# Routed-row scatters held behind TensorE signals, in a decoder layer with mixture-of-experts routing on one Trainium2 core

## What is computed

```
x = x + linear_attention_block(layernorm(x))        # incl. its own FFN with gelu
x = x + cross_attention(layernorm(x), ctx)          # 16 heads of 8, 77 keys a batch, softmax
x = x + moe(layernorm(x))
# moe: logits = xf @ gate_w.T; probs = softmax; top_p, top_i = top_k(probs, 2)
#      w = top_p / sum(top_p); rank = running count of tokens per (expert, choice)
#      keep = rank < capacity (1280); for each of 8 experts:
#      out += comb[:, e] * (silu(xf @ gate_e.T) * (xf @ up_e.T)) @ down_e.T
```

## Time and profile before

| | us |
|---|---|
| median of 3 runs (lowest, highest) | 974.47 (972.26, 980.99) |
| the profiled execution's own time | 977.34 |
| its span, first to last instruction | 975.5 |
| mean granted TensorE clock, share of full speed | 0.943 |
| TensorE matmul busy | 844.6 (87%) |
| VectorE busy | 641.7 (66%) |
| GpSimd busy | 539.9 (55%) |
| ScalarE busy | 453.3 (46%) |
| the 128 scatters of L852, busy on GpSimd | 129.6 |

### The profile page before, as it was taken

One profiled execution on the slowest core, in us unless ns is written; L12 is line 12 of the kernel. 1 busy time (PEld: TensorE's weight loads), 2 busy tenths in 40 slices (PEclk: granted clock), 3 DMA queues, 4 the chain that ended last, 5 costly groups with the idle time before them and its releaser, 6 DMA issues.

```text
span 975.5 us, 25508 instructions
## 1 busy us (share of the span) xinstructions
PE 844.6 (87%) x9107; PEld 625.8 (64%) x9107; DVE 641.7 (66%) x2064; ACT 453.3 (46%) x708; POOL 539.9 (55%) x747
## 2 busy tenths in 40 slices
PE   4799999999999999999999999862789889979883
PEld 3577787787667776666766667741456656656661
DVE  5888988988567877777777776734244544434443
ACT  1466766766367666666666655521222222222220
POOL 3465665665532366666655655565356656565565
PEclk8899999999999999999999998955799999989997
DMA  6369930000000011110000000100433344546440
GB/s 234 98 238 390 388 123 0 0 1 1 1 2 14 25 58 57 57 41 31 28 28 30 28 30 26 55 29 32 156 106 131 115 134 108 157 126 198 135 154 3
DMA packets 50336, 87.01 MB, mean 89 GB/s; under 512 B 12809, under 2 KB 28105, under 8 KB 50232
## 3 DMA queue, kind: packets, MB, share of 16 engines
q1 hardware_dynamic: 37872, 72.18, 22.0%
q0 software_dynamic: 11264, 12.70, 4.0%
q10 hardware_dynamic: 1096, 0.73, 0.2%
HBM read 42.08 MB, written 58.41 MB: 103 GB/s over the span
## 4 chain that ended last, share of the span: by engine, by line
PE 48%; DVE 8%; another core or an unknown queue 8%; issue 7%; ACT 3%; POOL 2%; DMA 1%; DVEq 0%; SPq 0%; POOLq 0%; ACTq 0%
PE psum L1398 6%; PE psum L1418 6%; PE psum L1880 6%; PE psum L1383 5%; PE psum L1892 5%; PE psum L1388 3%; PE psum L1429 2%; PE psum L1401 2%; DVE h L1832 2%; PE psum L1365 2%; DVE yo L1817 2%; PE psum L1369 1%; ACT num L1269 1%; PE psum L626 1%
## 5 line engine op out<-in xcount | busy, mean ns | idle before, releaser
L1779 POOL DMA_INDIRECT out<-yo,token x160 | 158.7, 992 | 123.3 <-issue 108.4
L852 POOL DMA_INDIRECT dispatched<-z,idx x128 | 129.6, 1013 | 72.7 <-issue 47.0
L1261 ACT ACTIVATE PT<-psum,key_bias 77x2048 f32<-77x2048 f32 x64 | 125.5, 1961 | 74.9 <-PE psum L1401 74.9
L1861 ACT ACTIVATE act_g<-psum 128x512 f32<-128x512 f32 x80 | 46.1, 596 | 191.2 <-DVE h L1832 95.3
L1398 PE MATMUL psum<-qT,Kb 32*77 32x128 f32 x2048 | 126.8, 282 | 0.8 <-issue 0.8
L951 DVE TENSOR_REDUCE top_score<-psum 128x8 f32<-128x616 f32 x128 | 101.6, 794 | 29.7 <-PE psum L1383 27.2
L1817 DVE SCALAR_TENSOR_TENSOR yo<-psum,xin,base 128x128 f32<-128x128 f32 x156 | 44.0, 343 | 111.6 <-remote 65.6
L1892 PE MATMUL psum<-down,h 128*128 128x128 f32 x640 | 85.5, 290 | 28.9 <-DVE h L1832 24.8
L1383 PE MATMUL psum<-Kb,qT 32*128 32x308 f32 x512 | 101.5, 471 | 0.8 <-ACT z3T L1252 0.4
L1892 PEld LDWEIGHTS psum<-down,h 128*128 128x128 f32 x640 | 80.0, 203 | 33.9 <-DVE h L1832 29.3
L1401 PE MATMUL psum<-MT,minus_sel 32*77 32x128 bf16 x1024 | 97.3, 217 | 2.3 <-issue 2.3
(11 more groups left out here) (177 smaller groups left out, 1743.5 us busy)
## 6 DMA issues: line engine op xcount, KB each, us to landing
dispatched<-zeros SPq DMA_DIRECT2D x40, 522.0 KB, 7.3
xin<-dispatched SPq DMA_DIRECT2D x40, 522.0 KB
out<-zeros SPq DMA_DIRECT2D x20, 256.0 KB, 3.1
first<-out SPq DMA_DIRECT2D x20, 256.0 KB
X<-in_x SPq DMA_DIRECT2D x16, 256.0 KB, 2.6
out<-X SPq DMA_DIRECT2D x16, 256.0 KB
out<-yo,token POOLq DMA_INDIRECT x160
ctx<-in_ctxT SPq DMA_DIRECT2D x4, 616.0 KB, 6.3
```

The costliest lines, as they stand in the source:

```text
L852: pool.indirect_dma_start(xg[k], bass.IndirectOffsetOnAxis(ap=idx[n % Z4][:, t, k:k + 1], axis=0), z4[n % Z4][:, t, :], None, bounds_check ...
L1261: nc.scalar.activation(PT[j % 2][:], T.rearrange("p a c -> p (a c)"), ACT.Exp, bias=key_bias[:, bass.ds(b, 1)]).then_inc(s["PT_ready"], 1)
L1779: pool.indirect_dma_start(rows_out if slot else out, bass.IndirectOffsetOnAxis(ap=token[i][:, t:t + 1], axis=0), yo[i][:, t, :], None, bou ...
```

## The change

In the loop, the first choice's scatter now also waits for the batch's complete shifted scores (`T_ps` = 4b + 4), and the second choice's waits for the turned numerators (`OT_ps` = b) where it waited for `MT_ps` = b + 2. `add_out_bias` moves from j = 2 to j = 3. After the loop, the scatters of groups 13 and 14 each stand behind one of several TensorE signals; those of group 15 and the place of `ln_scale` of group 15 stay.

```diff
                     if group(n):
                         if j == 0:
                             scatter_ready(n)
+                        pool.wait_ge(s["T_ps"], 4 * b + 4)
                         scatter_rows(n, j, 0)
 ...
-                    if j == 2:
+                    if j == 3:
                         add_out_bias(g)
                     if group(n):
-                        if batch(b + 1):
-                            pool.wait_ge(s["MT_ps"], b + 2)
+                        pool.wait_ge(s["OT_ps"], b)
                         scatter_rows(n, j, 1)
 ...
             def last():
                 scatter_ready(NG - 3)
-                for u in range(G4):
-                    for k in range(K2):
-                        scatter_rows(NG - 3, u, k)
+                pool.wait_ge(s["T_ps"], 4 * NB)
+                scatter_rows(NG - 3, 0, 0)
+                pool.wait_ge(s["z4T_ps"], NG - 1)
+                scatter_rows(NG - 3, 0, 1)
+                pool.wait_ge(s["pv_ps"], 8 * (NB - 1))
+                scatter_rows(NG - 3, 1, 0)
+                pool.wait_ge(s["gate_ps"], NG - 1)
+                scatter_rows(NG - 3, 1, 1)
+                pool.wait_ge(s["OT_ps"], NB - 1)
+                scatter_rows(NG - 3, 2, 0)
+                pool.wait_ge(s["pv_ps"], 8 * NB)
+                scatter_rows(NG - 3, 2, 1)
+                pool.wait_ge(s["OT_ps"], NB)
+                scatter_rows(NG - 3, 3, 0)
+                pool.wait_ge(s["oT_ps"], NG)
+                scatter_rows(NG - 3, 3, 1)
                 ln_scale(NG - 1, 4, mom4, var4, rs4, shift4)
-                for n in (NG - 2, NG - 1):
-                    scatter_ready(n)
-                    for k in range(K2):
-                        for u in range(G4):
-                            scatter_rows(n, u, k)
+                scatter_ready(NG - 2)
+                scatter_rows(NG - 2, 0, 0)
+                scatter_rows(NG - 2, 1, 0)
+                pool.wait_ge(s["z4T_ps"], NG)
+                scatter_rows(NG - 2, 2, 0)
+                scatter_rows(NG - 2, 3, 0)
+                pool.wait_ge(s["gate_ps"], NG)
+                scatter_rows(NG - 2, 0, 1)
+                scatter_rows(NG - 2, 1, 1)
+                pool.wait_ge(s["rank_ps"], NG)
+                scatter_rows(NG - 2, 2, 1)
+                scatter_rows(NG - 2, 3, 1)
+                scatter_ready(NG - 1)
+                for k in range(K2):
+                    for u in range(G4):
+                        scatter_rows(NG - 1, u, k)
```

## The result

The changed kernel takes 1001.94 us (median of 4 runs, 999.04 to 1003.63) where the kernel before takes 973.59 beside it: a ratio of 1.0295, 95% interval 1.025 to 1.034. The forecast was 966.0 with a range up to 982, so the sign is wrong and the time lies far outside the range. The profiled execution took 1003.63 with a span of 1001.8, 26.3 us more than before.

What follows compares the result with a forecast made beforehand. TensorE held 48% of the chain, with scatters thought to delay its signals, 2.9 us a group. Loop -6, tail -3 and +0.5 gave -8.5 us: 977.3 to 968.8 profiled, median 966.0, range 953 to 982.

Steps and rivals of the forecast that it cites:

- Costs nothing itself: In the loop, moving add_out_bias out of j = 2 is free, since add_out needs its result only three steps later.
- V and j = 0: ScalarE's V idles well under 1 us, not 1.62; j = 0's exponential comes less than 6.5 us behind the one before.
- The exponentials of j = 1 and j = 3: Sign of being right: they come about 0.5 us later after their shifted scores began, with periods unchanged.
- signs that I had named for being right: V's short idle, j = 0's earlier exponential, later exponentials at j = 1 and 3, num's last tail wait under 5 us.
- the idle time before `num` covers the late exponentials: On ScalarE, idle of 0.59 us (j = 3) and 1.37 (j = 1) before num absorbs exponentials 0.5 us late, costing 0.
- the loop's -6 us: Over 12 loop groups, V starting sooner at j = 0 saves 0.5 us each; bounds 0 and 19 us.
- My own bound of 0.5 us for this place: Upper bound per moved second choice amid the shifted scores, where the exponentials come late; the estimate was 0.
- Rival 3: In the loop, three second choices amid the shifted scores each cost 0.5 us, 19 us in all: 987 us; chance 0.15.
- The tail: After the loop, spread scatters bring the moments 3 us sooner; group 14's scatters then come 0.5 us later.
- Rival 4: A scatter's place does nothing to TensorE; the waits only add GpSimd's lag: 975 us; chance 0.05.

Runs made afterwards that it cites:

- the residual behind: Changed kernel with add_out_bias at j = 3 moved behind the second choice's scatter, against the kernel before: 988.21 us, 1.0115 (975 kind); 906.17 us, 1.0035 (902 kind).

## Why the prediction was wrong

1. *"Costs nothing itself"*, of `add_out_bias` out of j = 2: **this is the step that failed.** I asked who needs its result, and not what runs on VectorE while it runs. I had worked out its new place, 1.0 us behind the start of the first choice of j = 3 (measured 1.16), nose to tail behind a scatter, and that place is where VectorE does the ranks of the routing. The trace of before even shows the price once, at the end of the loop, where the residual of the last group (637.75 to 639.01) and the ranks meet: the view of `taken` there has 1234 ns as its longest beside a median of 158. The runs give the meeting its price: 1.27 us a group and 12.4 us in all on the 902 kind, 17.6 us on the 975 kind, and with the residual back at j = 2 a ratio of 0.9971 instead of 1.03 on the 975 kind. On the 975 kind it takes both moves: the wait on `OT_ps` shifts it by the 1.0 us that I had worked out, and that is more than `o` has to spare once it is held.

2. *The half clock.* None of my terms had it. Before, TensorE idles 1.92 us in a group in pieces; now 1.12 us of idle time in one piece precede most falls. A full-clock group takes 25.4 us, one with 6.8 us at the lower level 27.0, so the clock is 1.6 us of the 3.1 us by which the loop's period grew. That the collision brings most of them is what the counts say: 11 and 9 stretches in the loop in the two profiles of the changed kernel on the 975 kind, six with the residual behind, none and one with it at j = 2 (the second with the old tail), and one, two and four where the loop is that of the kernel before. That the idle piece is the cause is my reading, and not a rule: on the 902 kind pieces of 0.83 us (in the group of 425.76) went by without a fall in one run, and two stretches came in another of the same kernel.

3. *V and j = 0.* Right in kind: V idles 0.29 us, and the first choice of j = 3 moved by 0.9 us in its step (3.9 to 4.8), where I had 1.0. The exponentials of j = 1 and j = 3 come about 0.5 us later after their shifted scores began (2.53 and 2.56 us, where they had 2.00 and 2.10), as forecast. So most signs that I had named for being right came, in a kernel that got slower: none of them looked at VectorE. The step table, from the first matmul of the shifted scores to the next batch's, groups at full clock:

| step | before (batches 28 to 31) | changed (20 to 23) | residual back at j = 2 (28 to 31) |
|---|---|---|---|
| j = 0 | 6.61 | 7.34 | 5.91 |
| j = 1 | 6.14 | 5.88 | 6.15 |
| j = 2 | 5.78 | 6.23 | 5.92 |
| j = 3 | 5.49 | 5.98 | 5.99 |
| sum | 24.02 | 25.43 | 23.97 |

Without the collision, j = 0 gains 0.7 us. But j = 3 loses 0.5: that the idle time before `num` covers the late exponentials was wrong as well, and so the loop's -6 us came to nothing (286.7 us from batch 12 to 60 with the residual at j = 2, 287.2 before). The exponentials were not the only thing held. With the wait alone, TensorE's own timeline has a pause amid the shifted scores of j = 3, while the scatter of 425.18 runs:

```profile
425.78 0.41 PE L1397 MATMUL psum<-qT,Kb 32*77 32x128 f32 x3
426.47 0.32 PE L1397 MATMUL psum<-qT,Kb 32*77 32x128 f32 x1 [0.28 <-issue]
```

The weighing moves back by 0.7 us (from 2.99 to 3.70 us into the step) and `num` by 0.4, so the idle time that I had taken as cover is still there, 0.49 us of it, only later. My own bound of 0.5 us for this place had the right size. Rival 3 named the place, but its price of 19 us needed all three steps to lose, and only j = 3 does in the runs without the collision.

4. *The tail.* The sign was right, the size is not settled: from the last batch's first shifted score to the third stage the changed kernel is 6.7 us sooner in its first profile and 2.8 in its second, where I had 2.5. Since kernels with the old order are 4.7 and 5.5 us sooner too, the profiles do not say what the new order is worth. In the first profile the last `num` idles 4.58 us and the moments come 20.4 us behind those scores instead of 27.2:

```profile
683.35 0.38 ACT L1297 ACTIVATE num<-psum 128x256 f32<-128x256 f32 x1 [4.58 <-remote]
```

5. *The rivals.* Rival 4, that the place of a scatter does nothing to TensorE, had 5% and is, as far as TensorE's signals go, what the chips of the 902 kind do. The Trainium skill, "SBUF — State Buffer", section "SBUF: two separate sides", names the shared port pair of VectorE and GpSimd as an exclusive lock. The trace agrees for `xb`, under which `taken` takes 1.07 us and not 0.16, and that half of the rule was the one that decided. I had used only the other half, that TensorE waits on nobody. Here the traces agree on one kind of chip (1.97 us from shifted scores to exponential) and not on the other (2.59).

## What to carry to other kernels

When an elementwise operation of GpSimd is moved, look at VectorE's timeline over its new place before calling it free, and at what is nose to tail ahead of it. Two edits that each gain can meet: add the shifts of a queue, then ask again of each operation behind it what it now overlaps. Time that hides a delay is no cover if the same stall moves the work behind it too, so check what else the stall touches (here the dispatch of TensorE, not only its signal).

## What the runs showed of the hardware that I had not expected

- Two kinds of chip: the same kernel before takes about 975 us on some (medians 973.6, 975.0, 974.8) and about 902 on others (903.3, 901.8, 902.2). On the second kind no scatter was seen to hold TensorE's signals, and the changed kernel loses 1.7 to 2.2% instead of 3.0%. The wait and the tail gained 0.5 to 0.7% each on the first kind, and together lost 0.4% on the second; where those 0.4% lie stays open, since there is no profile of the kernel before from there.
- A small VectorE instruction that starts 0.33 us or more into a scatter with `xb` (128x512) right behind it ends with `xb`, after 1.6 to 2.1 us (11 groups or more in each of the six runs that have both edits, and in the one with the residual alone). Without `xb` behind it, one started 0.38 us into a scatter took its 0.17 us. It is not so for every operation of GpSimd behind the scatter: with the 128x4 `minus_mean` (L839) right behind, instructions of the ranks started 0.32 to 0.39 us into it took 0.17 us. Why `xb` differs, no run shows.
- A scatter with another scatter 0.3 us behind it can hold VectorE too, but only to its own end. The kernel before has this in eight groups of its loop, which I had overlooked; in the group of the earlier trace rows the instruction behind `taken` (GpSimd's scatter first, then VectorE):

```profile
401.57 1.12 POOL L852 DMA_INDIRECT dispatched<-z,idx  x1 [0.53 <-issue]
402.24 0.42 DVE L1066 TENSOR_SCALAR z<-rank 128x4 f32<-128x4 f32 x1
```

It starts 0.67 us into the scatter, takes 0.42 us for 0.16 and ends at 402.66, the scatter at 402.69.
- Of the changed kernel's loop groups on the 975 kind, those with full clock and those with a 6.8 us stretch at half clock differ by 1.6 us, 25.4 and 27.0, with the same work and order of events.
